# The epsilon of the last norm's variance moves from GpSimd to VectorE

## The reference

```python
h = _L0_tok_ref(x, ...)                                  # norm, 768 -> 192, norm
h = _layernorm(h + _L0_attn_ref(h, ...), axis=-1)        # channel attention, 8 heads of 24
h = _layernorm(h + _L0_ffn_ref(h, ...), axis=-1)         # soft mixture of 8 experts x 4 slots
```

```python
def _layernorm(x, axis=-1, eps=1e-05):
    m = jnp.mean(x, axis=axis, keepdims=True)
    v = jnp.var(x, axis=axis, keepdims=True)
    return (x - m) / jnp.sqrt(v + eps)
```

## Time and profile before

| | us |
|---|---|
| median of 3 runs | 111.77 |
| lowest, highest | 111.56, 112.86 |
| the profiled execution, its own time | 112.18 |
| its span, first to last instruction | 110.4 |
| TensorE matmuls busy | 101.7 (92%) |
| VectorE busy | 87.7 (79%), 380 instructions |
| ScalarE busy | 67.5 (61%) |
| GpSimd busy | 53.4 (48%), 126 instructions |

### The profile page before, as it was taken

How to read it: one execution, slowest core, us unless ns; L and a number is a source line. 1 busy time by engine, 2 the same in 40 slices (tenths; PEclk the granted TensorE clock), 3 DMA queues, 4 the chain that set the end, 5 groups by cost and what they waited for, 6 DMA issues and landing times. The chain is left out here.

```text
span 110.4 us, 4479 instructions
## 1 busy us (share of the span) xinstructions
PE 101.7 (92%) x1607; PEld 88.2 (80%) x1607; DVE 87.7 (79%) x380; ACT 67.5 (61%) x222; POOL 53.4 (48%) x126
## 2 busy tenths in 40 slices
PE   6999999999999999999999999799989989999900
PEld 6999989979999887887898887679779668879500
DVE  2129756968998958958977989999999897999960
ACT  4000023729563887798887996787785994476570
POOL 8800552263999887847204417906030340076880
PEclk9999999999999999999999999999999999999996
DMA  2999999469501111111000000010042000002232
GB/s 23 334 339 394 389 386 398 153 212 342 235 0 30 36 32 40 29 35 32 6 3 6 0 6 0 6 48 24 30 105 72 7 0 3 0 6 84 66 112 58
DMA packets 8554, 11.27 MB, mean 102 GB/s; under 512 B 2358, under 2 KB 5878, under 8 KB 8534
## 3 DMA queue, kind: packets, MB, share of 16 engines
q1 hardware_dynamic: 8533, 11.00, 29.5%
HBM read 9.22 MB, written 0.88 MB: 92 GB/s over the span
## 5 line engine op out<-in xcount | busy, mean ns | idle before, releaser
L480 PE MATMUL ps<-wc,xT 128*128 128x192 f32 x108 | 19.1, 330 | 0.0
L480 PEld LDWEIGHTS ps<-wc,xT 128*128 128x128 f32 x108 | 17.4, 190 | 0.7 <-issue 0.6
L1046 ACT ACTIVATE hT<-ps,b,g 128x128 f32<-128x128 f32 x18 | 7.3, 463 | 16.4 <-PE ps L491 16.3
L1068 ACT ACTIVATE km<-ps,imgsel 108x192 f32<-108x192 f32 (+1 forms) x32 | 11.1, 420 | 3.7 <-PE ps L515 3.6
L1256 POOL TENSOR_SCALAR mv<-mv 108x1 f32<-108x1 f32 (+1 forms) x11 | 3.0, 270 | 14.4 <-DVE mv L856 14.4
L568 PE MATMUL ps<-wp,yT 128*108 128x192 f32 (+1 forms) x44 | 9.3, 333 | 0.0
L664 PE MATMUL ps<-wu,hb 128*96 128x192 f32 (+1 forms) x44 | 9.2, 332 | 0.1
L1261 POOL TENSOR_TENSOR r<-mv,halves 108x2 f32<-108x2 f32 (+1 forms) x11 | 8.8, 803 | 0.8
L508 PE MATMUL ps<-wqk,hT 128*108 128x192 f32 (+1 forms) x44 | 9.0, 326 | 0.0
L726 DVE BATCH_NORM_STATS2 st<-xs 128x6 f32<-128x384 f32 x18 | 8.9, 537 | 0.0
L1249 POOL TENSOR_TENSOR rqt<-rn,tempc 128x6 f32<-128x6 f32 x11 | 2.2, 199 | 12.1 <-ACT rn L1105 12.1
(11 more groups left out here) (118 smaller groups left out, 296.6 us busy)
## 6 DMA issues: line engine op xcount, KB each, us to landing
xT<-in_x_t SPq DMA_DIRECT2D x9, 384.0 KB, 6.4
xs<-in_x SPq DMA_DIRECT2D x9, 384.0 KB, 6.2
out<-o SPq DMA_DIRECT2D x10, 81.0 KB
wt<-in_w_tok SPq DMA_DIRECT2D x2, 288.0 KB, 3.2
wqk<-in_w_qk SPq DMA_DIRECT2D x1, 192.0 KB, 5.9
wp<-in_w_proj SPq DMA_DIRECT2D x1, 192.0 KB, 10.0
wd<-in_w_down SPq DMA_DIRECT2D x1, 192.0 KB
z<-h SPq DMA_DIRECT2D x2, 81.0 KB
```

The costliest lines, as they stand in the source:

```text
L480: mm = pe.matmul(tokp(t), xT[:, o + kc * 128:o + (kc + 1) * 128], wc[:, kc, :], start=kc == 0, stop=kc == KC - 1)
L1046: ins = act.activation(hT[:, f, t * 128:(t + 1) * 128], htp(t)[:, f, :], ACT.Identity, bias=b2[:, f:f + 1], scale=g2[:, f:f + 1])
L1068: act.activation(km[0:n, g % NK, i, :], qkp(g)[:, 1, :], ACT.Copy, scale=imgsel[0:n, i:i + 1])
```

## The change

GpSimd's ln4_root loses its addition and the wait in front of it, and keeps the power. VectorE gets a new step last_var(g), which adds the same constant to the same numbers into the same tile and signals the same semaphore `var4_ready`. It stands right behind last_moments(g) in VectorE's list, in all eleven groups. The order of all other calls is as before.

```diff
+            def last_var(g):
+                n = tokens(g)
+                dve.wait_ge(mv4_ready, g + 1)
+                dve.tensor_scalar(var4[0:n, g:g + 1], mv4[0:n, g, 1:2], EPS_LN, None, ALU.add).then_inc(var4_ready, 1)
+
             def last_out(g):
...
-            last_residual(1); slot_bias(4); last_moments(0); take_d(10); last_stats(1); last_residual(2)
-            last_stats(2); last_moments(1); last_residual(3); last_shift(0); last_moments(2)
-            last_stats(3); last_residual(4); last_moments(3); last_shift(1); last_stats(4); slot_bias(5)
-            last_shift(2); last_moments(4); spread(1); slot_bias(6); last_residual(5); slot_bias(7)
-            last_stats(5); last_residual(6); last_shift(3); last_moments(5); last_stats(6); slot_bias(8)
-            last_residual(7); last_moments(6); last_shift(4); last_stats(7); slot_bias(9)
-            last_residual(8); last_moments(7); last_shift(5); last_stats(8); slot_bias(10)
-            last_moments(8); last_residual(9); last_shift(6); last_stats(9); last_shift(7)
-            last_moments(9); last_residual(10); last_shift(8); last_stats(10); last_moments(10)
-            last_shift(9); last_out(10)
+            last_residual(1); slot_bias(4); last_moments(0); last_var(0); take_d(10); last_stats(1)
+            last_residual(2); last_stats(2); last_moments(1); last_var(1); last_residual(3)
+            last_shift(0); last_moments(2); last_var(2); last_stats(3); last_residual(4)
+            last_moments(3); last_var(3); last_shift(1); last_stats(4); slot_bias(5); last_shift(2)
+            last_moments(4); last_var(4); spread(1); slot_bias(6); last_residual(5); slot_bias(7)
+            last_stats(5); last_residual(6); last_shift(3); last_moments(5); last_var(5); last_stats(6)
+            slot_bias(8); last_residual(7); last_moments(6); last_var(6); last_shift(4); last_stats(7)
+            slot_bias(9); last_residual(8); last_moments(7); last_var(7); last_shift(5); last_stats(8)
+            slot_bias(10); last_moments(8); last_var(8); last_residual(9); last_shift(6); last_stats(9)
+            last_shift(7); last_moments(9); last_var(9); last_residual(10); last_shift(8)
+            last_stats(10); last_moments(10); last_var(10); last_shift(9); last_out(10)
...
             def ln4_root(g):
                 n = tokens(g)
-                pool.wait_ge(mv4_ready, g + 1)
-                pool.tensor_scalar(var4[0:n, g:g + 1], mv4[0:n, g, 1:2], EPS_LN, None,
-                                   ALU.add).then_inc(var4_ready, 1)
                 pool.wait_ge(var4_ready, g + 1)
                 pool.tensor_tensor(rstd4[0:n, g:g + 1], var4[0:n, g:g + 1], mhalf[0:n, 0:1],
                                    ALU.pow).then_inc(rstd4_ready, 1)
```

## The result

The changed kernel takes 113.41 us (median of 14 executions, 112.52 to 113.93), the kernel before, beside it, 111.84 (median of 14, 111.32 to 112.86). The ratio is 1.0117, with a 95% interval of 1.009 to 1.0143: slower by 1.2%, clear of noise, and inside the two per cent that the prediction calls "same". The prediction said 112.9, range 112.0 to 113.8, a ratio of 1.010.

The account below looks back on a forecast made before the run. VectorE's list was taken as the bound: 0.04 + 8 x 0.18 - 0.08 - 0.10, by unrounded starts 1.28, less 0.13 gives +1.15 us; forecast 112.9 us, ratio 1.010, range 112.0 to 113.8.

Parts of the forecast that it names:

- What bounds the stage: Last stage: VectorE's list of calls, busy 8.68 of 8.90 us, carries it; GpSimd's queue only keeps up.
- Group price, 0.18: Behind last_moments on VectorE: the next call starts 0.27 after it instead of 0.09, 0.18 us per group if nothing covers it.
- the pointer form: One-element tensor_scalar with a pointer operand on VectorE: upper bound for the addition, 0.21 us with a spacing of 0.13.
- Groups 0 and 1: Additions ahead of VectorE calls that wait for TensorE: the waits hide most of the price, 0.04 us is left.
- The two places where delay dies: VectorE's last_shift(2) no longer waits for its power, 0.08 us; slot_bias(7) waits for slot_out(7) on TensorE, absorbing 0.10.
- The last step: Group 10, end of last_moments(10) to end of the power: 0.97 us becomes 0.84, a gain of 0.13.
- Rival A: GpSimd's queue is the real bound and VectorE has room: only the 0.13 gain, 111.6 us; chance 0.07.
- C: VectorE's wait overlaps other work, so each addition pays only 0.07 of issue: about +0.25 us, 112.0; chance 0.10.
- D: A dependent one-element VectorE call costs more, 0.32 us per group: +2.7, 114.5 us, slower by over 2%; chance 0.06.
- Rival B, the lock: VectorE's addition is held by a running GpSimd power; addition 2 would be held 0.16, giving 113.1 us; chance 0.07.
- The rule on chained calls: Skill page: VectorE's next operation waits for an empty pipe, semaphore or not; the change would then cost about +0.9 us.
- ScalarE's and the stores' share: Last stage: last_norm on ScalarE has gaps and shifts with the delay; the stores behind last_out stay as they are.

Follow-up runs that it names:

- the two one-sided kernels: Two runs against the kernel before: no addition anywhere, epsilon left out (ratio 0.9938); GpSimd untouched, VectorE also adding into an unread tile (ratio 1.0135).
- the doubled one: Changed kernel plus a second VectorE addition behind each last_var, waiting for the first and writing an unread tile: 116.63 us, ratio 1.0428.

## Why the prediction was right

The direction and the mechanism held; the size came out short. In the frame above the change costs +1.36 for a predicted +1.15. By the ratio it is +1.3 us (+1.0 to +1.6), and the two medians are 1.57 apart; what lies between these figures is not resolved. The parts of the sum:

- **What bounds the stage.** Right. VectorE's list did, not GpSimd's queue on which the chain ends. Shown by the two one-sided kernels: GpSimd's work without its additions moves last_moments(10) by 0.01, VectorE's with them by 1.54.
- **Group price, 0.18.** Mis-sized: last_moments(10) came 0.21 later for each of groups 2 to 9 on average (0.18 to 0.23). The call behind the addition starts 0.27 to 0.31 after the moments, where 0.27 was forecast; most of these starts lie 0.01 to 0.02 above it, as the wait is 0.03 to 0.04. The rest is a cost that the prediction put at nothing: a call that starts behind the addition, and no longer inside the moments, lets its own follower start later. last_shift(4) took 0.07 to the next start where it took 0.04 (102.78 to 102.82 before, shown above):

```profile
103.52 0.15 DVE L973 TENSOR_SCALAR var<-mv 108x1 f32<-108x1 f32 x1
103.58 0.15 DVE L985 SCALAR_TENSOR_TENSOR sh<-mv,rstd 108x1 f32<-108x1 f32 x1
103.65 0.35 DVE L963 BATCH_NORM_STATS2 st<-z 108x6 f32<-108x192 f32 x1
```

  Over eight groups the price accounts for nearly all of the missing 0.25. The addition itself took the predicted 0.15 (150 to 154 ns); the pointer form's 0.21 was not the nearest row.
- **Groups 0 and 1.** 0.04 was left, 0.06 measured (last_residual(3) 1.66 us behind last_moments(0), 1.60 before).
- **The two places where delay dies.** Right: 0.08 predicted and 0.09 measured at last_shift(2), 0.10 and 0.09 at slot_bias(7). The first rests on the spacing in the earlier trace rows, not on the wait of the earlier trace rows, which was last_shift(9)'s. slot_bias(7) started 5.20 us behind last_moments(0) for 4.71 before, +0.49 where 0.40 was forecast.
- **last_moments(10).** +1.28 forecast, +1.53 measured: 0.05 from groups 0 and 1 (as it stood at last_moments(2)), 1.66 from groups 2 to 9, less 0.18 at the two places.
- **The last step.** -0.13 forecast, -0.17 measured: the last power took 0.53 behind idle time, where it took 0.57 behind an addition.
- **Rival A** fell with the one-sided kernels, **C** with the 0.21 per group. C's price, 0.38 to last_moments(10), is about what the addition costs where it waits for nothing or where independent calls cover the wait (0.36 and 0.33). **D** did not occur.
- **Rival B, the lock.** Not seen. Where both engines add, VectorE's addition at 99.00 lies wholly inside GpSimd's power of 98.67 to 99.25 and takes the same 0.15:

```profile
98.67 0.58 POOL L1276 TENSOR_TENSOR rstd<-var,mhalf 108x1 f32<-108x1 f32 x1
...
99.00 0.15 DVE L974 TENSOR_SCALAR spare<-mv 108x1 f32<-108x1 f32 x1
```

  In the changed kernel no addition took more than 0.154.
- **The rule on chained calls.** The Trainium skill (VectorE: DVE Perf Modes, Rules for kernel authors) advises to minimize the count of operations and not the semaphores. Here eleven operations without a wait on their neighbour cost VectorE 0.36 us and eleven with it 1.54, so for calls this short the trace does not agree: the wait is what costs. The section that the prediction weighed (The DRAIN you can't avoid) also says that a next operation that is not held starts earlier, which the prediction left out and which the starts 0.09 into an instruction of 0.17 bear out.
- **ScalarE's and the stores' share.** Nothing of them came onto the path, as said.

## What to carry to other kernels

The engine on which the chain of waits ends is not necessarily the one that sets the pace: look at what released its last instruction, and at how full the engine behind that was. Moving a small dependent instruction onto a full engine cost mostly the wait for its operand (eleven cost VectorE 0.36 us without it and 1.54 with it). With one independent call between producer and consumer the 1.53 us of the changed kernel's additions fell to 0.61, and with a second where the first was too short, to 0.33. Relief of an engine that only keeps up is worth what it shortens behind the last link, here 0.17 us.

## What had not been expected of the hardware

TensorE's clock came into play at a distance: an idle time of 1.49 us, after work up to 98.86, was followed by about 3 us at a granted clock of 0.52, and keeping TensorE busy there gave 1.03 us back; an idle time of 0.81 at the same place was followed by 1.00. How long a gap may be between these two was not tried. Delay on VectorE thus cost in a straight line here only as long as TensorE's gap stayed short.

GpSimd's power of group 4 took 0.72 us in the changed kernel (at 100.35, shown above) and 0.91 in the doubled one, where the other powers of these two kernels' last stage take 0.53 to 0.55. Both ran beside VectorE's spread(1), a product of two SBUF tensors (0.48 us). The Trainium skill (SBUF — State Buffer, Who interferes with whom) has a VectorE instruction with two SBUF inputs contend with a GpSimd instruction that reads SBUF. The trace agrees as far as these two lengths go. But in the kernel before a power at 99.80 also ran beside spread(1) (99.72, 0.46 us) and took only 0.60, so what sets the length stays open. In the changed kernel it cost nothing, as nobody waited for that power.
